# A two-layer attention and expert kernel on one core: the order of each engine's steps written anew

## The chip, the cores and the metric

The kernel runs on 1 core of one Trainium2 chip. The metric is the device time of one execution in microseconds (us). A core has five engines that run side by side, each its own list of instructions in order: TensorE (PE, matrix products), VectorE (DVE), ScalarE (ACT), GpSimd (POOL), and SyncE (SP), which here only starts transfers (DMAs). They meet through semaphores: an instruction waits until a count is reached, and adds to one when it ends.

## The reference

```python
x = x + L0_xattn(layernorm(x), ctx)   # 16 heads of 8: q, k with an RMS norm per head, softmax, values, projection
x = x + L0_ffn(layernorm(x))          # int8-like quantised input, 128 -> 512, 3-tap conv along the sequence, silu, 512 -> 128
x = x + L1_xattn(layernorm(x), ctx)   # one head of 128, then a product with [x, output]
x = x + L1_ffn(layernorm(x))          # 8 experts: softmax(x @ gate); (silu(x @ Wg) * (x @ Wu)) @ Wd, weighted by the gate
```

x is 64 sequences of 128 rows of 128 float32 values, ctx 64 of 120 rows of 128. With 128 rows and a capacity of all of them, each expert takes every row.

## The kernel before

The 64 sequences go through in 16 groups of 4 (`SIZES`). Each group passes six stages, and a stage is a fixed list of steps on each engine (`steps_of`, L339):

- **n**: first layer norm (POOL: `ln1` = three small operations, L945, and `xn1` = four of L955), its transpose, q, k and v on PE (L565 to L586), the RMS roots on DVE (`rms` 1 to 9, L1066 and L1072 to L1079), then the copies `k_r` to `ql` on DVE (L1174 to L1197), `k_hi` on ACT (L840) and `dup_q`, `dup_k` on POOL (L975, L981). SP then transposes `kht`, `qht` and `ks` (L471 to L483) and spreads `kht` into `kbd` with 16 small DMAs for the first two sequences (`kbd0`).
- **m**: 16 steps `max`, four per sequence: one matmul into the only bank BM (L597), one reduction on DVE (L1202). SP's step of this stage (`kbd1`, L500) is the 16 DMAs for the other two sequences. A `max` of sequence 0 waits for its quarter of `kbd0`, one of sequence 2 for its quarter of `kbd1`.
- **a**: per sequence `stacks`, two `scores`, `values`, `turn` on PE with ACT copies and exponentials between them, and on DVE `rden` and `turn`; then `ont` and `proj`. POOL's step is `xres` (L991), which needs the input `xres` from a DMA.
- **b**: the feed-forward part: `quant` 0 to 4 on DVE (L1238 to L1251), transpose `xit`, four `fc1`, conv and silu, four `h2t`, and `fc2`, which waits for four DMA transposes `hit` (L517).
- **d**: the second attention: `xn3t`, `bf`, `s1`, `p1t`, `oc`, `fused`, `xn4t`, `gate` on PE.
- **c**: the experts, in 16 units: PE `g` (three matmuls into bank pg), `u` (three into pu), ACT tanh of pg (L915) and copy of pu (L931), DVE product (L1363, step `u`), POOL product (L1000, step `u`), PE `d` (L783), DVE sum (L1377). Bank pg is single: the next `g` waits for L1363 of the unit before.

**w** is the preparation of the weights, once: on DVE `wabs`, `wint`, `gate_w`, `wg`, `wu` (L1107 to L1135).

How the stages of different groups mix is written out by hand, as a string per engine in `ORDER`: each letter means "the next step of that stage" (`run`, L402), so a string fixes the engine's whole order, and within one stage the order never changes. In the middle part c of group g runs beside d of g+1, b of g+2, a of g+3 and m and n of g+3 to g+5; the strings repeat with a period of some 108 PE steps, one group. Before the first c there is only the rest to do (the fill), and at the end only c is left (the tail). `UNREAD` says at which of PE's steps, counted from 0, so many float32 products of 128x128 are made that nobody reads (L790); each shows as two matmul records in the trace.

Of the kernel before, what the change touches and what calls it, by code (L numbers as in the profile page):

```python
# [64 lines left out]
STAGES = "wnmabdc"  # L65
ORDER = {
    "sp": (
        "annnnmnnnnnnnnnmnnnnannmnbbnnnbbnanmdbbnbnnbnnanmdbbnbnbcnnnanmdbbbbncnnnnamdnbbbbnnnmcadnnnbbbbnnncamdnnnbb",
# [8 lines left out]
        "dbmcamccabcmccabnnmdacacdmbcmcccbcmccbamccamccbmccamccaaccbamccamcanaccaccdaadccdccccaccdccdcdbcaccbancabann",
        "mcbcdmcccdbccmaccacmcbaccaacbcamccabmccmccbmacmcaaccamccbamccamnamccaccdaadmccdmccmccaccdccdcdbcaccbancabann",
        "ccbdmcccdbccamccacmcbamccaacbcamccabmcccmcbamccaaccamccbamccamnamccaccdaadmccdmccmccamccdccdcdbcaccbancabann",
        "ccbdccmcdbccamccacmcbamccaacbcamccabmcccmcbamccaaccamccbamccamnamccaccdaadmccdmccmccamccdccdcdbcaccbancabann",  # L80
        "ccbdccmcdbccamccacmcbamccaacbcamccabmcccmcbamccaaccamccbamccamnamccaccdaadmccdmccmccamccdccdcdbcaccbancabann",
        "ccbdccmcdbccamccacmcbamccaacbcamccabmcccmcbamccaaccamccbamccamnamccaccdaadmccdmccmccamccdccdcdbcaccbancabann",
        "ccbdccmcdbccamccacmcbamccaacbcamccabmcccmcbamccaaccamccbamccamnamccaccdaadmccdmccmccamccdccdcdbcaccbancabann",
        "ccbdccmcdbccamccacmcbamccaacbcamccabmcccmcbamccaaccamccbamccamnamccaccdaadmccdmccmccamccdccdcdbcaccbancabann",
        "ccbdccmcdbccamccacmcbamccaacbcamccabmcccmcbamccaaccamccbamccamnamccaccdaadmccdmccmccamccdccdcdbcaccbaccabacc",
        "dcbcdccambccmcaccambcaacambcamccbmccmccabmcaccaccamcbamccamcamccacdadaccdmccmccamccdcmdccdbcaccbaccabaccdcbc",
# [10 lines left out]
        "ccdbcacbancbbabcnbdccncbbccadbcacacbcbacabcbcccbabcacbbaccacaccannaccdadcccdccacdccdbcacbancbbabcnbdccncbbcc",
        "adbcacacbcbacabcbcccbabcacbbaccacaccannaccdadcccdccacdccdbcacbancbbabcnbdccncbbccadbcacacbcbacabcbcccbabcacb",
        "baccacaccannaccdadcccdccacdccdbcacbancbbabcnbdccncbbccadbcacacbcbacabcbcccbabcacbbaccacaccannaccdadcccdccacd",
        "ccdbcacbancbbabcnbdccncbbccadbcacacbcbacabcbcccbabcacbbaccacaccannaccdadcccdccacdccdbcacbancbbabcnbdccncbbcc",  # L100
        "adbcacacbcbacabcbcccbabcacbbaccacaccannaccdadcccdccacdccdbcacbacbcbacdbcbcccbbacdcabcacababcbcbccabcbcacbbca",
# [18 lines left out]
        "ddbcdcbbacbbabmnbnbdbcdmbdnbcbmdnbccbdbdbmcanannnbnbnbcmnnnbmbnbcmnnbmbcbmncaacmcbmddmamanncncnabmbcdmdcmddb",  # L120
        "cbbcbcbddbcdcbbacbbabnnbnbdbcdmdnbbcbdmdbcdmcbmbnbncanannbnbnbcmnnnbmbnbcmnnbcbmbcaacmcbmddmamanncncnabmbcdm",
        "dcmddbcbmbcbcbddbcdcbbacbbabnnbnbdbcdmdnbbcbdmdbcdmcbmbnbncanannbnbnbcmnnnbmbnbcmnnbcbmbcaacmcbmddmamanncncn",
        "abmbcdmdcmddbcbmbcbcbddbcdcbbacbbabnnbnbdbcdmdnbbcbdmdbcdmcbmbnbncanannbnbnbcmnnnbmbnbcmnnbcbmbcaacmcbmddmam",
        "anncncnabmbcdmdcmddbcbmbcbcbddbcdcbbacbbabnnbnbdbcdmdnbbcbdmdbcdmcbmbnbncanannbnbnbcmnnnbmbnbcmnnbcbmbcaacmc",
        "bmddmamanncncnabmbcdmdcmddbcbmbcbcbddbcdcbbacbbabnnbnbdbcdmdnbbcbdmdbcdmcbmbnbncanannbnbnbcmnnnbmbnbcmnnbcbm",
        "bcaacmcbmddmamanncncnabmbcdmdcmddbcbmbcbcbddbcdcbbacbbabnnbnbdbcdmdnbbcbdmdbcdmcbmbnbncanannbnbnbcmnnnbmbnbc",
        "mnnbcbmbcaacmcbmddmamanncncnabmbcdmdcmddbcbmbcbcbddbcdcbbacbbabnnbnbdbcdmdnbbcbdmdbcdmcbmbnbncanannbnbnbcmnn",
        "nbmbnbcmnnbcbmbcaacmcbmddmamannccabmbcdmdcmddbcbmbcbcbddbcdcbbcbaabbcdbdbdbcmbbmbcdcbcdmbdbabambbbmcbmbbcmbc",
        "babamccmcbmddmamaccabbcdmdcmddbcbmbcbcbmddbcdcbbcbaabbcdbdbdbcbbcbcbcddbababdbbbcbbbcbbbcccaabdcdaaccabbccdd",
# [1287 lines left out]
```

How the kernel before makes its waits and increments, by code:

```python
            def do_n(name, t, c, g):  # L458
                n = size(g)
                if name == "xin" and g < NG - 1:
                    sp.wait_ge(xn1_done.sem, xn1_done.at(g))
                    sp.dma_start(xin[:, 0:size(g + 1), :], x_g(g + 1)).then_inc(xin_in.sem, 16)
                elif name == "ctxa" and g < NG - 1:
                    sp.wait_ge(v_ps.sem, v_ps.at(g))
                    sp.dma_start(ctxt_a[:, 0:size(g + 1), :], ctxt_g(g + 1)).then_inc(ctxa_in.sem, 16)
                elif name == "kht":
                    sp.wait_ge(kh_done.sem, kh_done.at(g))
                    if later(g):
                        for part in kbd_in[0] + kbd_in[1]:
                            sp.wait_ge(part.sem, part.at(g - 1, 16 * HQ))
                    sp.dma_start_transpose(kht[:, 0:n, :], heads(k_hi[:, 0:n, :])).then_inc(kht_in.sem, 16)
                elif name == "qht":
                    sp.wait_ge(q_hi_done.sem, q_hi_done.at(g))
                    if g >= 2:
                        sp.wait_ge(max_ps.sem, max_ps.at(g - 2, 4 * size(g - 2)))
                    sp.dma_start_transpose(qht2[:, g % 2, 0:n, :], heads(q_hi[:, 0:n, :])).then_inc(qht_in.sem, 16)
                elif name == "ks":
                    sp.wait_ge(dup_done.sem, dup_done.at(g, 2))
                    sp.wait_ge(kl_done.sem, kl_done.at(g))
                    if g >= 2:
                        sp.wait_ge(s_ps.sem, s_ps.at(g - 2, 2 * size(g - 2)))
```

## Time and profile before

| | |
|---|---|
| three runs | 1236.44, 1240.61 (median), 1243.52 us |
| the profiled execution | 1241.86 us, of it a span of 1239.9 us from the first to the last instruction |
| PE busy | 1118.7 us, 90% (of it unread products 53.7) |
| DVE busy | 1038.1 us, 84% |
| ACT busy | 836.3 us, 67% |
| POOL busy | 700.4 us, 56% |
| idle of PE in the first 62 us | 42.6 us |

A row of a group of instructions names the line, the engine, the operation, what is written and what is read, how many there are, the busy time and the mean of one in ns. `x4` in a timeline row means four instructions merged. What stands in square brackets is the idle time of the engine just before, and who ended it. DVE and ACT rows that follow each other can overlap by 0.1 us.

### The profile page before, as it was taken

The page shows a single profiled execution, that of the slowest core. Times are in us where ns is not written, and L with a number is a line of the kernel's source. Part 1 is how long each engine was busy: PE and PEld are TensorE (multiplying, and loading weights), DVE is VectorE, ACT ScalarE, POOL GpSimd, SP SyncE. Part 2 cuts the span into 40 slices and gives each one's busy share as a digit, 9 for nine tenths or more (in the row PEclk, how much of TensorE's full clock was granted, in tenths as well). Part 3 has the DMA queues.
Part 4 walks back from the last instruction along what each step waited for, and adds up shares of the span by engine and source line. Part 5 has one row for each costly group of instructions (what it writes and reads, how often), then busy time and mean ns, then how long its engine had stood idle before and what let it go on. Part 6 is the DMA issues. An engine that isn't in the chain of part 4 may idle for free.

```text
span 1239.9 us, 27832 instructions
## 1 busy us (share of the span) xinstructions
PE 1118.7 (90%) x10025; PEld 806.6 (65%) x10025; DVE 1038.1 (84%) x2728; ACT 836.3 (67%) x1685; POOL 700.4 (56%) x827
## 2 busy tenths in 40 slices
...
DMA packets 151399, 53.67 MB, mean 43 GB/s; under 512 B 116832, under 2 KB 150624, under 8 KB 150880
## 3 DMA queue, kind: packets, MB, share of 16 engines
...
q14 instruction: 54, 0.44, 0.1%
...
## 4 chain that ended last, share of the span: by engine, by line
DVE 38%; PE 32%; POOL 10%; issue 7%; ACT 6%; SPq 4%; DMA 2%; POOLq 0%; DVEq 0%
PE py L783 5%; DVE moe L1363 5%; DVE q_st L1202 5%; POOL xn L955 4%; SPq L498 3%; DVE h L1272 2%; DVE acc L1377 2%; DVE am L1277 2%; PE pa L633 2%; POOL moe L1000 2%; DVE xn L1251 2%; DVE cv L1266 2%; PE pg L773 2%; DVE cv L1261 2%; DVE rr L1079 2%
## 5 line engine op out<-in xcount | busy, mean ns | idle before, releaser
L1000 POOL TENSOR_TENSOR moe<-moe 128x512 f32<-128x512 f32 x256 | 331.4, 1296 | 369.1 <-ACT moe L931 223.6
L783 PEld LDWEIGHTS py<-wd_s,moe 128*128 128x128 f32 x1856 | 236.8, 192 | 28.4 <-DVE acc L1377 6.2
L783 PE MATMUL py<-wd_s,moe 128*128 128x128 f32 x1856 | 246.6, 277 | 4.1 <-DVE acc L1377 3.7
L1363 DVE SCALAR_TENSOR_TENSOR moe<-tg,pg 128x512 f32<-128x512 f32 x232 | 157.8, 680 | 41.0 <-ACT tg L915 39.0
L1202 DVE TENSOR_REDUCE q_st<-pa 128x4 f16<-128x480 f32 x256 | 168.0, 656 | 24.2 <-PE pa L597 24.1
L915 ACT ACTIVATE tg<-pg 128x512 f32<-128x512 f32 x232 | 139.5, 602 | 60.9 <-PE pg L775 58.5
L849 ACT ACTIVATE probs<-pa 120x512 f32<-120x512 f32 x256 | 139.5, 605 | 24.2 <-PE pa L623 24.0
L931 ACT ACTIVATE moe<-pu 128x512 f32<-128x512 f32 x232 | 140.7, 606 | 11.3 <-PE pu L775 8.6
L597 PE MATMUL pa<-kbd,qht 128*128 128x480 f16 x256 | 96.1, 375 | 20.9 <-DMA kbd<-kht 10.7
L773 PE MATMUL pg<-x4h,wg_h 128*128 128x512 f16 x232 | 88.8, 383 | 17.2 <-DVE moe L1363 17.0
L955 POOL TENSOR_SCALAR xn<-x,lnm,lnr 128x128 f32<-128x128 f32 x192 | 101.6, 542 | 1.5
L773 PE MATMUL pu<-x4h,wu_h 128*128 128x512 f16 x232 | 88.2, 380 | 0.0
L775 PE MATMUL pg<-x4h,wg_l 128*128 128x512 f16 x232 | 88.2, 380 | 0.0
L774 PE MATMUL pg<-x4l,wg_h 128*128 128x512 f16 x232 | 88.2, 380 | 0.0
L774 PE MATMUL pu<-x4l,wu_h 128*128 128x512 f16 x232 | 87.9, 379 | 0.0
L775 PE MATMUL pu<-x4h,wu_l 128*128 128x512 f16 x232 | 87.9, 379 | 0.0
L633 PE MATMUL pa<-probs,v_st 120*9 120x128 f32 x2048 | 70.0, 275 | 1.0 <-ACT probs L849 0.5
L950 POOL TENSOR_TENSOR lnr<-lnv,half 128x4 f32<-128x4 f32 x64 | 66.3, 1036 | 0.0
L873 ACT ACTIVATE hr<-pb,magic,sc 128x512 f32<-128x512 f32 x64 | 49.9, 780 | 24.1 <-DVE sc L1283 23.6
L633 PEld LDWEIGHTS pa<-probs,v_st 120*9 120x9 f32 x2048 | 49.3, 91 | 19.1 <-issue 14.3
L597 PEld LDWEIGHTS pa<-kbd,qht 128*128 128x128 f16 x256 | 24.9, 97 | 56.7 <-DVE q_st L1202 17.8
L1377 DVE SCALAR_TENSOR_TENSOR acc<-py,aff,acc 128x128 f32<-128x128 f32 x208 | 58.2, 341 | 3.8 <-PE py L783 3.7
...
## 6 DMA issues: line engine op xcount, KB each, us to landing
kbd<-kht SPq DMA_DIRECT2D x512, 3.8 KB
...
```

The lines of the kernel that those rows point to most:

```text
L633: mm = pe.matmul(pa[32 * n:32 * n + HD + 1, BO, i * S:(i + 1) * S], v_st[0:SC, t, HQ * n + i, :], probs[0:SC, i, n, :], start=True, stop=True)
L773: pe.matmul(o, w_hi[:, us], x4h, start=True, stop=False)
L774: pe.matmul(o, w_hi[:, us], x4l, start=False, stop=False)
L775: pe.matmul(o, w_lo[:, us], x4h, start=False, stop=True).then_inc(done.sem, 1)
L783: mm = pe.matmul(moe_y(g, e)[:, j, :], hu[:, u % 3, j * S:(j + 1) * S], wd_s[:, u, :], start=(half == 0 and j == 0), stop=(half == 1), ski ...
L849: act.activation(probs[0:SC, i, :, :], pa[0:SC, i % 2, :], ACT.Exp).then_inc(p_done.sem, 1)
L915: act.activation(tg[:, u % 2, 0:wide], moe_bank("g", g, u)[:, 0:wide], ACT.Tanh, scale=0.5 / WSCALE)\
L931: act.activation(us[:, u % 3, 0:wide], moe_bank("u", g, u)[:, 0:wide], ACT.Copy, scale=0.5 / WSCALE ** 2)\
L955: ins = pool.tensor_scalar(dst[:, j, :], src[:, j, :], lnm[:, i, j:j + 1], lnr[:, i, j:j + 1], ALU.add, ALU.mult)
L1000: pool.tensor_tensor(hu[:, u % 3, 0:wide], gw[:, u % 3, 0:wide], us[:, u % 3, 0:wide], ALU.mult)\
L1202: dve.tensor_reduce(q_st2[:, g % 2, t, 4 * c:4 * c + 4, 3 * HD], pa[:, BM, 0:4 * SC].rearrange("p (h k) -> p h k", h=4), AX.X, ALU.max, ne ...
L1363: dve.scalar_tensor_tensor(out=gw[:, u % 3, 0:wide], in0=tg[:, u % 2, 0:wide], scalar=1.0, in1=moe_bank("g", g, u)[:, 0:wide], op0=ALU.add ...
```

## The change

All ORDER strings are replaced, and UNREAD is: 162 unread products in 59 places become 166 in 53, the last of them before PE's step 158 and not 165. No instruction of the computation is added or dropped: PE keeps its 1731 steps, ACT 1300, POOL 496, DVE 1845, SP 224. What is different in them, read off with `steps_of`:

- POOL at the start: `ln1, xres, xn1, dup_q, dup_k` of group 0 becomes `ln1, xn1, dup_q, dup_k`; `xres` of group 0 comes after `xn1` of group 2.
- DVE at the start: `wabs` before `ln1`; `gate_w` goes between the roots of group 0, `wg` to after `qb` of group 1, `wu` to after the last `max` of group 0. In the string of before all of these stand ahead of `qb` of group 0.
- SP at the start: `kht, qht, kbd1, ks, kbd0` of group 0 becomes `kht, qht, ks, kbd0, xin, ctxa, kbd1`.
- PE: `stacks` of group 0 comes after 10 of its `max` steps and not after 4; the first `max` comes before k and v of group 1.
- The first `g` is PE's step 162 and not 168, the second group's 284 and not 285, then (before/after) 393/392, 504/510, 609/619, and the last group's 1683/1682.
- In the middle, `proj` to `xit` of a group is 24 PE steps before and 60 after; `fc2` to `xn3t` 15 and 50; from the step ahead of ACT's `k_hi` to the first `max` of the same group 52 and (groups 8 to 11 and 13) 37. SP's order there differs from group to group: groups 8, 9, 10, 13 and 15 have `kbd1` before `ks` and `kbd0`, with `kht` just ahead of it or `qht` between; the others have `kbd0` first.
- In the middle the steps between `g` of unit 1 and `g` of unit 2 were `u, s1, max`; now they are `u, turn, stacks`.

```diff
--- before.py
+++ after.py
@@ -40,7 +40,7 @@
-UNREAD = {1: 2, 2: 3, 3: 3, 4: 3, 6: 3, 7: 3, 8: 3, 11: 3, 12: 3, 13: 3, 14: 3, 15: 3, 16: 3, 18: 3, 20: 1, 32: 3, 34: 3, 37: 2, 39: 3, 41: 3, 43: 2, 46: 2, 48: 3, 50: 3, 52: 1, 58: 3, 59: 3, 60: 3, 62: 3, 64: 3, 66: 3, 74: 3, 75: 3, 76: 2, 84: 3, 88: 3, 90: 1, 94: 3, 98: 3, 100: 3, 102: 2, 109: 3, 113: 3, 116: 2, 117: 3, 118: 3, 119: 3, 120: 3, 129: 3, 131: 3, 133: 3, 135: 3, 144: 3, 148: 3, 153: 2, 158: 3, 161: 3, 163: 3, 165: 2}
+UNREAD = {1: 4, 2: 3, 3: 4, 4: 3, 7: 4, 8: 3, 11: 4, 12: 4, 14: 4, 15: 4, 16: 4, 17: 3, 18: 3, 19: 3, 25: 3, 27: 4, 31: 2, 33: 3, 35: 4, 39: 2, 41: 3, 43: 4, 47: 2, 49: 3, 51: 4, 59: 4, 60: 3, 63: 4, 65: 2, 70: 2, 71: 3, 78: 3, 81: 3, 88: 3, 92: 4, 95: 3, 100: 2, 102: 3, 113: 4, 115: 3, 118: 3, 119: 3, 121: 4, 123: 2, 126: 3, 128: 2, 135: 3, 138: 3, 139: 1, 142: 4, 147: 2, 156: 3, 158: 3}
...
@@ -65,69 +65,69 @@
     "sp": (
-        "annnnmnnnnnnnnnmnnnnannmnbbnnnbbnanmdbbnbnnbnnanmdbbnbnbcnnnanmdbbbbncnnnnamdnbbbbnnnmcadnnnbbbbnnncamdnnnbb",
-        "bbnnncamdnnnbbbbnnncamdnnnbbbbnnncamdnnnbbbbnnncamdnnnbbbbnnncamdnnnbbbbnnncamdnnnnbbbbnncaamdnnbbbbcdbbbbcd",
-        "dbbbcbcc",
+        "nnnnnnnnmnnnannmnannnnmbbnnnnbbnnmbbbndbnnannnmbbbnnabncnadnnmdbbbbnnnnnnmacbbndbbnnnmnncbnbbbandnmannncbnbb",
+        "nbdnmnannnnbdcbbbnnmnnbbannbcbanndnnmbbbnbcncndnnnmbndabnbbnmnnnnbabcbnbcndnnnmbbanbbnncdmnnnbadbbbbcbdbbcbb",
+        "bdbcdacc",
     ),
     "pe": (
-        "wwwnnnnnnnnmmmmaammamamnaanmnmamammamaaammamamaaammamamnammaaaamamnamnaanmmmbmambamambaaambamambaaamambamnab",
-        "mabaaambammmmnmbnmnmaaamamadadmadabmmbamdmbdmdbmaabaaamdmbmdccambcamcbanmccbaccaaccaccacbccccanmcanncaccamcc",
...
+        "wwwnnnnnnmnmmnmmmmmmnmnnaamamamaaamamamaaamamamaaamamamnmamamammnanmnmamaambaabmamaabmaambamabmmamambaambama",
+        "mbnambamammmbnannmamaadmadadmbmbmadmbdmdbmaambaaammdmbcdmccabmacbaaccabccacamnaccabcaaccaccacamccaaccacmccdm",
...
     ),
     "act": (
-        "wwwwnnnnnnnnnnaaaanannaaaaaaaaaaannaaaanaanbnabaabbaabbaabbaabaabnbbabnabababbnaannaadadabdbadbbdbbaabbaabdc",
...
+        "wwnwwnnnnnnnnnnaanaanaaaaaaaaaaaannananaanababaabababbabbaabababababnnbbabbnannaaaddabdbadbbdbbaabbaabdcbbdc",
...
     ),
     "pool": (
-        "nannnnnnnnnnnnanbbnnnnadbdbdddncccncncncabcbdcddcccccccncddccnccnncabcbdcddcccccccddccnccccccdnccdbcbcdcancn",
-        "cdcdcccccccccdcddccanbcbccncnncddcccccccccnccdcddccabcbcncncncddcccccccccnccdcddccabcbcncncncddcccccccccnccd",
...
+        "nnnnnnnnnnannnnabbnnnnaddbbdddccncnccadbcbcdndcccncccddcccccccccddcbacbcncncnccndcddcccccccnnccdaccbdbcnccnd",
+        "ccddccccccccccbbdcccdcndnccncnccddccccccaccdcacbbccccndncndccncccddcccccccdccabcbccncdccncdnncccddcccccccdca",
...
     ),
     "dve": (
-        "nwnwwwwnnnnnnnnnnnnnnnnnnnnnnnnnnnnnnnnnnnnnnnnmmmmnnmmmmaanmnmnmnnmnnmnnmnnanannmnmnmnmaammmmamanmnnnabbmmm",
-        "nbababmbmbmnmbmnnbmbmnbababmnnbbmbmnbababmnbmnbnbnbmnnababmbnnnbbnbnnbmbnbmmmmmbmadbdbmnanamnnmnnnnnbnbnbnbm",
...
+        "wnnwnnnnnnnwnnnnnnnnnnnnnnnwnnmnnnnnnmnnnnnnnmnnnmnmnmmmmmnnmnmmannnnnmanmnmwnmanammnnnnnaammmmannamnnmambmb",
+        "nmnbbmbnbmbnmnnbnannanmnnbnbmnbmbabmbabbmnmbbmbmbmbbbaambnbbmbmbabamnnbbbnmnmnmmbadbdnbnmnnnnnnnmmbbanbbbndm",
...
     ),
```

## Rows read from the trace of the kernel before

**Rows 1.** The page: busy time of each engine.
```profile
PE 1118.7 (90%) x10025; PEld 806.6 (65%) x10025; DVE 1038.1 (84%) x2728; ACT 836.3 (67%) x1685; POOL 700.4 (56%) x827
```
**Rows 2.** Stretches: length; busy (count) of PE, PEld, DVE, ACT, POOL; PEclk; DMA; GB/s.
```profile
34.30:194.90 160.60, 125.84 (x1263) 97.82 (x1264) 128.07 (x333) 74.05 (x134) 43.48 (x69) 0.91 0.20 46
155.00:186.00 31.00, 26.41 (x282) 19.44 (x283) 29.71 (x84) 16.13 (x34) 8.84 (x16) 1.00 0.16 39
556.80:626.50 69.70, 66.32 (x608) 47.23 (x609) 63.52 (x171) 51.66 (x106) 43.67 (x52) 1.00 0.22 42
768.90:841.30 72.40, 66.40 (x608) 47.09 (x608) 63.75 (x171) 51.68 (x106) 43.62 (x52) 1.00 0.20 44
```
**Rows 3.** What PE waited for, whole span: us in total, times, longest.
```profile
PE pa L565 <- POOL xn L955: 21.7, 2, 12.4
PE pg L773 <- DVE moe L1363: 17.0, 33, 1.1
PE pa L597 <- DMA kbd<-kht: 10.7, 5, 6.2
PE pb L664 <- DVE xn L1251: 7.5, 13, 1.7
```
**Rows 4.** Timeline of POOL and DVE at the start (start, length).
```profile
18.57 1.03 POOL L950 TENSOR_TENSOR lnr<-lnv,half 128x4 f32<-128x4 f32 x1
22.93 1.26 POOL L991 TENSOR_TENSOR xres_b<-xres,bp_s 128x512 f32<-128x512 f32 x1 [3.33 <-DMA xres<-in_x]
24.18 5.96 POOL L955 TENSOR_SCALAR xn<-xin,lnm,lnr 128x128 f32<-128x128 f32 x4
...
26.34 2.28 DVE L1135 SCALAR_TENSOR_TENSOR wu_l<-moe,wu_h 128x2048 f16<-128x2048 f32 x1
```
**Rows 5.** Timeline of SP, groups 0 and 1.
```profile
45.46 11.79 SPq L498 DMA_DIRECT2D kbd<-kht  x16
...
59.08 11.65 SPq L498 DMA_DIRECT2D kbd<-kht  x16
```
**Rows 6.** Timeline of PE and DVE: the first `max` steps, the first `stacks`, `proj` of group 0.
```profile
63.13 0.58 PE L597 MATMUL pa<-kbd,qht 128*128 128x480 f16 x1 [6.25 <-DMA kbd<-kht]
73.51 0.63 PE L609 MATMUL pa<-id_h,q_st 128*128 128x128 f16 x4
107.38 1.16 PE L654 MATMUL pa<-wp_s,on_t 128*128 128x128 f32 x8
...
77.31 0.66 DVE L1202 TENSOR_REDUCE q_st<-pa 128x4 f16<-128x480 f32 x1 [0.47 <-PE pa L597]
```
**Rows 7.** Timeline and two stretches around the longest wait in the middle.
```profile
353.18 3.71 DVE L1242 TENSOR_SCALAR am<-am 128x4 f32<-128x4 f32 x1
...
355.60 1.27 POOL L991 TENSOR_TENSOR xres_b<-xres,bp_s 128x512 f32<-128x512 f32 x1
...
359.31 0.61 PE L623 MATMUL pa<-st_t,ks_t 32*128 32x128 f16 x8 [2.96 <-ACT p L895]
...
361.00:366.00 5.00, 5.00 (x43) 2.59 (x42) 3.17 (x6) 2.25 (x5) 2.92 (x5) 0.55 0.03 5
```
**Rows 8.** Two groups of DVE instructions: busy us, mean ns; then idle before.
```profile
L1242 DVE TENSOR_SCALAR am<-am 128x4 f32<-128x4 f32 x16 | 15.2, 947 | 0.0
L1280 DVE TENSOR_SCALAR am<-am 128x1 f32<-128x1 f32 x64 | 9.3, 145 | 0.3
```
**Rows 9.** Timeline: one hand-over of bank pg.
```profile
497.95 0.68 DVE L1363 SCALAR_TENSOR_TENSOR moe<-tg,pg 128x512 f32<-128x512 f32 x1
...
498.68 0.39 PE L773 MATMUL pg<-x4h,wg_h 128*128 128x512 f16 x1 [0.44 <-DVE moe L1363]
498.91 0.38 PE L774 MATMUL pg<-x4l,wg_h 128*128 128x512 f16 x1
...
499.54 0.60 ACT L915 ACTIVATE tg<-pg 128x512 f32<-128x512 f32 x1 [0.66 <-PE pg L775]
```
**Rows 10.** DMA issues: how many, median us from issue to landing.
```profile
kht<-k_hi SPq DMA_TRANSPOSE x16, 2.4
```

More of the change, by code:

```diff
@@ L77 @@
[L77 to L86, printed above, removed]
@@ new lines @@
+        "cacbcacadbcdnaabdccamcbmacannaadbcccdmccbamccambanacmcbaccaacmamcbcmccmcacmccamcacaccacmcdmcdmccmdcccbmcccbm",
+        "ccamcbadncmdbaacdbcaccamamnanbacdmccbccmdcmcabmcacmbacnacmcccacbacacmacamamcaacamccacaccaaccaccbdccbdcccdbcc",
+        "cacabdnaacdmbcdcmacbmacmancbmnamdcbcadcaaccambcccmaccmccmcbmccccmncmcccmamcaacaccamaccaaccaccacabaacbacccdbc",
+        "dccdbccccbccamanccdmabdcmdbacnmanbmnccdacbccdmcamccmccmbccacmccmccmcccmamcaacmaccamaccaacaccacabcaacbacccdbc",
+        "cdcdbccccbccamaccndmabdcmdbacnnmabmnccdacbcdcmcamcccmcbcmccmcacmccmcccmamcaacmaccamaccaacaccacabcaacbacccdbc",
@@ new lines @@
+        "cdcbcdccccbcamancdcamdbcmdbacnmnambnccdacbcdcmcamccmccmbcccamccmccmcccmamcaacmaccamacacaccaccaabcaacbacccdbc",
+        "dccdbcccccbcamaccdnambdmcdbacnnmabmnccdcbacdcmcamccmccabcmccmccmccmcccmamcaacaccamacmcaaccaccacabcaabacccdbc",
+        "dccdbcccmbccacadccmandbcmdbacnmnabmnccdcbacdcmcamccmccbcmccamccmccmcccmamcaacamccamaccaaccacacabcaacbacccdbc",
+        "dccbcdccbccacmacdcnmdabcmdbacnmnabmnccdacbccdmcamccmccbmcccamccmccmcccmamcaacmaccamaccaaccaccacabaacbacccdbc",
+        "dccdbcccccbcamaccdnmbdmacdbacnmanbmnccdcabcdcmcamccmccbcmccmcacmccmcccmamcaacmaccamacaaccaccacabcaacbacccdbc",
@@ L89 @@
+        "cdcccbdcccbccamcadcdambdcabcmcacbcccmcbadccmcdcamccmbcacccmcccmamcaaccacmcacadcmdaacdmcccbmccmbaccacmabcdaac",
+        "dbccdbcaccacaccbdacbdcaccacbcccccbccccccccbcccccccccccccccccbcccbdcccdbcccdccccbcccdcccbdccdcbccccbccccbdccc",
+        "dcbcccccccccbccccccccccdccccdccdccccccdccdccccdccccccccccdccccccccdccccccccccccccccccccccccccccccccccccccccc",
         "ccc",
@@ L97 @@
[L97 to L101, printed above, removed]
@@ new lines @@
+        "bbcaabacnacbdbcnccbcdabbaccbabncbccaccacaaanacaccacaccacacbdcbdccbcdbcacbabdnacbdbbcacabccabnbdcbcanabdcbcac",
+        "bcbccccaccccnccaaacacacncaccaacabacbaccbdbcdcbbccbdbcaccbadndccbacbbnbnncbdbcacbdbcaccccccccacccaaacacacncac",
+        "acacabcabaccbdbcdcbbccbdbcaccbadccdnbbacbnnbncbdaccbbdbcaccccccacccccaaacacacnaccacacabacbaccbdbcdbbcccbdbca",
+        "acbdcdcnbcbacbnnbncbdaccbbdbcacccccaccccccaaacacacncaccaacabcabaccbdbcdcbbccbdbcacabcdcdncbacbbbnnncbdbcacbd",
+        "cbaccccacccccccaaacacaccaccanacabcabaccbdbcdbcbccbdbcacabdcdcbbcnacbnbnncbdbcacbdbcaccccccacccccaaacacacncac",
@@ L104 @@
+        "acacabcabaccbdbcdbbcccbdbcacbadcdncbcacbbnnbncbdacbcbdbcaccccccacccccaaacacaccnaccacacababaccbdbcdbcbccbdbca",
+        "cabdccdnbbcacbnbnncbdcacbbdbcaccccccacccccaaacacacnaccacacabcabaccbdbccdbcbccbdcbacdbacdbcabcbcbccbcbcadbcbc",
+        "cdcaccaccccaacaccadaccdacccbdcabcababdccbadbccbbaccabccacdbbdacbbcccbcbcccbcbccccccccccccccccbcbcdccbbdccdbc",
+        "cbcccdbcccbdcbccbccbcbccbdcbccdbcbbcccccccccccdccdcccccdcdcccdcccccccccccdcccccdcccccccccccccccccccccccccccc",
         "cccc",
@@ L120 @@
[L120 to L129, printed above, removed]
@@ new lines @@
+        "bcbbbdaamdbdmbcbnbnnbdbcbndmdncbnbabmacdnbnbmncnabdnamnnbbbndnncnmmnbmccdmdcanmcmbbcancmacnmbbbmbmcbccdbmcdb",
+        "mbdmdbbbmcbaabbcdbdbbdmcmbncbabbnanmdbbcmdbdnmcbbbmnnnbndbmdbcnaandcmcnncbanbmndbdmnnmcncnnaabcnbbmcbbcancbc",
+        "bbcaddbcbbddbcbbacmbbbdabmmbdbdbmncbmbbanmadcdbbndbcnndncnbmbbncnnmmdcdnmcmbcmcnddmacmbnmabacncnmbcbnabcabnn",
+        "bcnbncbnbcaabbcbcdbbcbdbbdbcdmbmbbaabmcdbdbcdbmnnbmbnbncdbbcbddmnndmcndndmncbmdcmcmcadmcnnmbmnbaacmncmnncbaa",
+        "nbcbbnbnncbncbbncbbacbcdbbcbdbaddcbbmbmcbbabamdbdbcdbnmnbmbnbncdbcbnbddmdnnmcnndmdncbmdcmcmcndmacnmbmbnnanam",
```

34 lines of the change are left out of this document (16 added, 18 removed).

## The prediction

> **What bounds the kernel now.** First the busy times [rows 1]: PE works 90% of the span, and the change takes no matmul away. What can be gained is the 121 us in which PE is idle, and the 53.7 us of unread products, which only stand where PE would wait. Then the stretches [rows 2]. In the fill (34.3 to 194.9) DVE is busy 128.1 of 160.6 us and PE 125.8, much of it unread products; from 155 to 186 DVE is busy 29.7 of 31 us. In the middle both are near full: PE 66.3 and DVE 63.5 of a period of 69.7 us. So in the middle no order can save more than 3.4 us a period; but the same order repeated gives one period of 72.4 us with the same 66.4 us of PE work. Third, PE's waits [rows 3]. The largest is at the start, 21.7 us for POOL's `xn1` of groups 0 and 1. Then come many small ones on DVE's hand-over of bank pg (17.0 in 33), waits for `kbd` (10.7 in 5), and `xit` waiting for `quant` (7.5 in 13).
>
> Two places show what the two engines do to each other. At 24.18 POOL's four `xn1` operations take 5.96 us, while DVE runs two operations of 2.28 us, the second of them shown [rows 4]. At 353.18 a DVE operation on four numbers per partition takes 3.71 us, while POOL runs on from one operation to the next, one of them the `xres_b` at 355.60 [rows 7]; that form's mean is 0.95 us [rows 8]. PE then waits 2.96 us, and afterwards a stretch of 5 us runs at a granted clock of 0.55, which is about the lower of the two levels, 1.2 GHz [rows 7].
>
> The Trainium skill (SBUF — State Buffer, section "SBUF: two separate sides") says that VectorE and GpSimd share a port pair which the one that starts first holds for its whole instruction. It would hold the tiny operation back for what was left of one GpSimd operation. The trace disagrees in size: the wait went over three of POOL's, the last of them ending at 356.87. By the rule the stall at 353 would be some 1.3 us and not 3.6, and the term for it below about -1 in place of -4.
>
> **The change, term by term**, against the profiled execution's 1241.9 us (span 1239.9; the median of the three runs, 1240.6, is 1.3 lower).
>
> 1. *Start.* POOL's roots end at 19.60; `xn1` then stood behind `xres`, whose DMA was late, until 24.18, and behind DVE's `wg` and `wu`, until 30.14 [rows 4]. With `xres` moved behind and `wg`, `wu` moved to later, `xn1` starts at about 20.5 (DVE's `ln1` now comes after `wabs`, I allow 0.9) and ends at about 24, 6 us earlier. The cover is gone for `wg` and `wu`: their 4.6 us on DVE now stand beside groups 1 and 2. ACT's two weight copies come between `xn1t` and `qsq`; I allow 0.4.
>    On SP `kbd1` of group 0 took 11.79 us ahead of `ks` and `kbd0` [rows 5]. Now `ks` can go at about 40 and `kbd0` at 42, and 4.05 us later (59.08 to 63.13 in rows 5 and 6) PE's first `max` starts: at 46, not 63.1.
>    That isn't a gain of 17. `stacks` of group 0 now comes after ten `max`; the ninth and tenth need `kbd1`, issued behind `kbd0` and two inputs from about 55, so 62 by SP. By DVE it is later: in its order group 1's roots and copies, `wg` and the ten `max` (1.13 us from one to the next, the 0.66 and 0.47 of rows 6) stand ahead: I count 71, against 73.5 [rows 6], 2.5 earlier. From there to `proj` (33.9 us before [rows 6]) there are 15 `max` and not 20, up to 0.66 us each: 3.3, of which I take 2.5. DVE has done the same work by `proj` of group 0 in both orders, and from there to the first `g` it is nearly full, so what is gained there stays. Term: **-5**. Bounds: -12 if SP decides (stacks at 62), and -1 if DVE's later `wu` and `wg` use the gain up.
> 2. *The stall at 353.* Without it PE's 2.96 us wait goes, and of 5 us at 0.55 [rows 7] the 2.3 us that the lower clock cost. In the new string `quant` of that group stands beside other POOL steps. Term: **-4**, bounds 0 (it comes up elsewhere) and -6. What is late next is the hand-over of pg.
> 3. *Other blocking in the middle.* The tiny L1242 takes 0.95 us where one like it, L1280, takes 0.15 [rows 8]: 16 times 0.8 is 13 us of held DVE, and other operations on SBUF alone are held too. Only where PE waits for DVE is it worth anything. Going by the two periods, 69.7 and 72.4 [rows 2], I take **-2**, bounds -7 (three slow periods gone) and +3 (one more).
> 4. *More room before `xit` and `xn3t`.* `proj` to `xit` goes from 24 PE steps to 60 and `fc2` to `xn3t` from 15 to 50, at 69.7/108 = 0.65 us a step 23 and 22 us more. The 7.5 us of waits for `quant` [rows 3] have no reason left in the middle. Term: **-4**, bounds 0 and -7.5.
> 5. *Less room for bank pg.* From the end of `g` to the next `g` the chain needs 0.16 (0.39 less the 0.23 from one start to the next), 0.60 on ACT, 0.68 on DVE and some 0.1 between them, 1.55 us [rows 9]. With `u, turn, stacks` between, PE has 0.66 for `u` and an estimated 0.44 and 0.22 for the other two (512 columns each, the first in float32, at twice the price), 1.3 us of work: 0.25 short, once a period, and in some groups twice. I take 0.3 in 13 groups: **+4**, bounds 0 (ACT and DVE are late anyway) and +6.
> 6. *Unread products.* Four more, 53.7/162 = 0.33 us each, 1.3 us at most; they stand in waits for `kbd` and in group 0. **0**, bounds 0 and +1.3.
> 7. *The rest:* PE's own step counts to the second and last `g` differ by one, and the tail has only c in it: 0. SP's changed places I cost at nothing; their cover is the first rival.
>
> Sum: -5 - 4 - 2 - 4 + 4 = -11, so 1241.9 - 11 = **1231 us**.
>
> **Rivals.**
> *A, slower: `kbd` late in the middle.* In groups 8, 9, 10, 13 and 15 SP issues `kbd1` ahead of `ks` and `kbd0`, and PE's distance from the `k_hi` to the first `max` shrinks from 52 steps to 36 to 38: 23.9 us, not 33.5. Needed are 2.4 for `kht` to land [rows 10], 11.8 for `kbd1`, 1.8 for each of `qht` and `ks` (the gap between the two `kbd` rows, 57.25 to 59.08, in which `ks` was issued), and 4.05 to the first quarter of `kbd0` [rows 5, 6]: 21.9. The margin is 2 us. It decides as soon as something holds SP by more, since SP's queue is in order and stands behind `ctxa` and the `hit` steps. A wait of 3 us and 1 us for the clock after it, five times, is +20: 1251. For it: PE already waited for `kbd` 10.7 us in all [rows 3]. Against it: `kht` goes long after the `hit` steps before it.
> *B, nothing gained:* the start's gain is used up by DVE, which is full in the fill [rows 2], and the waits only change places: term 1 at -1, 2 to 4 at -4 together, 5 at +4: 1241. For it: 63.5 of 69.7 us of DVE [rows 2].
> *C, more:* SP decides at the start (-12), the stall and all slow periods go (-6 and -7), pg costs nothing and `xit`'s waits go by half: sum -12 - 6 - 7 + 0 - 4 = -29 at its end; half-way between this and the forecast, 1221. For it: the places named are where POOL and DVE meet.
> That the order on the chip isn't the one in the strings can't be: each engine runs its list in order.
>
> **How the numbers follow.** Forecast 0.50, with a range of its own of 1223 to 1238; A 0.14; B 0.21; C 0.15. This kernel's runs can tell 0.5% (6.2 us) from no change, so faster is under 1234.4, slower over 1246.8. Faster: all of C, and 0.42 of the forecast's 0.50: 0.57. Slower: A, 0.14. The rest 0.29. The range 1216 to 1247 leaves out A's centre and C's far end.
>
> **What would show it.** Term 1: PE's first `max` near 46 us, `xn` L955 of group 0 under 4 us, `proj` of group 0 (107.4) near 102. Term 2: no DVE operation of over 3 us, no stretch at a clock of 0.55 after 100 us. Term 3: L1242's mean under 0.6 us. Term 4: `pb L664 <- xn L1251` under 3 us. Term 5: `pg L773 <- moe L1363` stays at 15 or more. A: waits of `pa L597 <- kbd` of 2 us and more after 600 us. The prediction is wrong if periods of the middle are over 71 us on the mean, or if the first `g` comes no earlier than before.

## The result and the profile after

| | median | runs |
|---|---|---|
| before | 1240.51 us | 7, 1236.44 to 1244.42 |
| after | 1232.37 us | 7, 1230.12 to 1234.82 |

The ratio is 0.9936, 95% interval 0.9914 to 0.9959: 8.1 us shorter, faster by the bound of 0.5%. The forecast was 1231. The profiled execution took 1234.4 us with a span of 1232.5.

The page of the changed kernel, busy time of each engine, against [rows 1]:

```profile
PE 1122.8 (91%) x10033; PEld 805.9 (65%) x10033; DVE 1043.8 (85%) x2728; ACT 836.8 (68%) x1685; POOL 695.4 (56%) x827
```

Stretches of the changed kernel, columns as in [rows 2]: the fill up to the first product of the experts, the first stretch of DVE near its limit, and the two periods that answer to those of before:

```profile
34.30:186.50 152.20, 121.34 (x1182) 91.16 (x1182) 125.56 (x316) 69.29 (x125) 41.17 (x68) 0.93 0.20 42
155.00:186.00 31.00, 26.05 (x252) 17.43 (x253) 29.07 (x72) 18.61 (x38) 9.66 (x19) 1.00 0.02 4
552.30:628.80 76.50, 68.77 (x609) 49.00 (x607) 66.80 (x171) 51.89 (x105) 44.16 (x52) 0.96 0.21 40
768.80:839.00 70.20, 66.58 (x611) 46.56 (x607) 64.24 (x170) 51.73 (x105) 44.38 (x52) 1.00 0.25 51
```

The first product of the experts comes 8.4 us earlier. The period that took 72.4 takes 70.2, but the one that took 69.7 takes 76.5, at a mean clock of 0.96: a stall that before didn't have. From the start of the span to that first product, before and after:

```profile
0.00:194.88 194.88, 135.00 (x1302) 106.42 (x1304) 143.48 (x364) 80.11 (x140) 57.86 (x87) 0.90 0.27 71
0.00:186.48 186.48, 135.74 (x1251) 104.42 (x1251) 147.37 (x360) 76.94 (x134) 53.29 (x86) 0.93 0.27 68
```

PE is idle for 59.9 us of it before and for 50.7 after, 9.1 less. Over the whole span its idle time falls from 121.2 to 109.7 us, 11.5 less, and its busy time grows by 4.1. So in these two executions only 2.4 us of the idle time saved lie behind the first product.

What PE waited for, against [rows 3]:

```profile
PE pb L664 <- DVE xn L1251: 15.7, 14, 2.5
PE pa L597 <- DVE q_st L1202: 13.9, 20, 2.9
...
PE pa L565 <- POOL xn L955: 13.1, 2, 11.1
PE pg L773 <- DVE moe L1363: 12.7, 16, 3.2
```

The start's wait fell from 21.7 to 13.1 and that for `kbd` from 10.7 to 1.9 in two. The wait for bank pg fell too. The wait of `xit` for `quant` (L1251), which was to go, has doubled, and that of `max` for DVE's reduction (L1202) grew from 9.0 us to 13.9.

The start of the changed kernel, POOL and DVE, against [rows 4]:

```profile
19.29 2.67 POOL L955 TENSOR_SCALAR xn<-xin,lnm,lnr 128x128 f32<-128x128 f32 x4
...
21.68 7.00 DVE L1125 TENSOR_SCALAR w_i<-hr 128x512 f16<-128x512 f32 x1
21.91 6.49 POOL L970 MEMSET kbd<- 128x7680 f16 x1
```

`xn1` is 2.67 us long and ends 8 us earlier. But POOL's clearing of the `kbd` tiles now lies beside DVE's L1125, which takes 7.00 us; its twin at 20.23 took 0.56. SP and then PE, against [rows 5, 6]:

```profile
41.81 11.81 SPq L498 DMA_DIRECT2D kbd<-kht  x16
...
58.07 11.65 SPq L498 DMA_DIRECT2D kbd<-kht  x16
```

```profile
47.43 0.37 PE L597 MATMUL pa<-kbd,qht 128*128 128x480 f16 x1
...
70.44 0.39 PE L609 MATMUL pa<-id_h,q_st 128*128 128x128 f16 x4
...
101.32 1.23 PE L654 MATMUL pa<-wp_s,on_t 128*128 128x128 f32 x8
```

The first `max` is 15.7 us earlier, `stacks` 3.1 and `proj` 6.1.

### Where the middle gave it back

The stall at 353 is gone, with its stretch at 0.55 [rows 7]. Around 604 the changed kernel has another. SP's queue, ACT, DVE and PE there, and the stretch behind it:

```profile
596.84 1.22 SPq L517 DMA_TRANSPOSE hi_t<-hq  x1
598.11 0.58 SPq L523 DMA_DIRECT2D ctxt_b<-in_ctx_t  x1
598.73 2.02 SPq L524 DMA_DIRECT2D ctxn_b<-in_ctx  x1
600.80 0.46 SPq L528 DMA_DIRECT2D out_x<-acc  x1
601.31 6.39 SPq L517 DMA_TRANSPOSE hi_t<-hq  x3
...
605.76 0.72 ACT L881 ACTIVATE hq<-hr,unmagic 128x512 f16<-128x512 f32 x1 [2.06 <-DMA hi_t<-hq]
...
607.00 0.69 DVE L1363 SCALAR_TENSOR_TENSOR moe<-tg,pg 128x512 f32<-128x512 f32 x1 [2.05 <-ACT tg L915]
...
607.74 0.61 PE L773 MATMUL pg<-x4h,wg_h 128*128 128x512 f16 x1 [3.18 <-DVE moe L1363]
```

```profile
608.00:616.00 8.00, 8.00 (x43) 5.39 (x42) 5.54 (x17) 3.49 (x9) 3.75 (x3) 0.65 0.05 9
608.00:613.00 5.00, 5.00 (x26) 3.23 (x25) 3.07 (x9) 2.54 (x7) 3.50 (x3) 0.50 0.07 15
```

To be read upwards: PE waits 3.18 us for the product that frees bank pg; DVE waits for ACT's tanh; ACT's tanh stands behind `hq`, which waits for a `hit` transpose to release its buffer. SP had put three transfers between the first transpose and the second, which went at 601.31 and not at about 598.1. PE did not work for 3.18 us, and then ran 8 us at a granted clock of 0.65, the first 5 of them at 0.50, the lower of the two levels. The periods, of both kernels in their profiles: from the first unit of group 3 to that of group 10 the changed kernel takes (910.3 - 409.1)/7 = 71.6 us a period, the kernel before (910.9 - 418.5)/7 = 70.3. Some 0.5 us of this difference is no loss: by the strings PE has 757 steps between these two points and had 752, at 0.65 us a step.

### The profile page after: what moved, and what is told of

Same layout as the page of the kernel before. It is cut to its first block, busy times and chain, and to the rows that moved or that the text cites. A ratio compares the mean times of both kernels' runs of the same rounds, so it can differ in the third digit from the quotient of the medians.

```text
span 1232.5 us, 27848 instructions
## 1 busy us (share of the span) xinstructions
PE 1122.8 (91%) x10033; PEld 805.9 (65%) x10033; DVE 1043.8 (85%) x2728; ACT 836.8 (68%) x1685; POOL 695.4 (56%) x827
## 4 chain that ended last, share of the span: by engine, by line
PE 57%; DVE 28%; ACT 6%; issue 3%; SPq 2%; POOL 2%; DMA 1%; POOLq 0%; DVEq 0%; ACTq 0%
PE py L783 11%; PE pg L773 3%; PE pa L597 3%; DVE moe L1363 3%; DVE q_st L1202 3%; PE pg L775 3%; PE pg L774 3%; PE pu L773 3%; PE pu L775 3%; PE pu L774 3%; PE pa L633 3%; DVE xn L1251 2%; PE pb L680 2%; ACT probs L849 2%; DVE h L1272 2%
## 5 line engine op out<-in xcount | busy, mean ns | idle before, releaser
L783 PEld LDWEIGHTS py<-wd_s,moe 128*128 128x128 f32 x1856 | 236.4, 192 | 26.5 <-issue 3.9
L783 PE MATMUL py<-wd_s,moe 128*128 128x128 f32 x1856 | 250.1, 278 | 3.0 <-ACT side L927 1.7
L1202 DVE TENSOR_REDUCE q_st<-pa 128x4 f16<-128x480 f32 x256 | 168.0, 656 | 24.8 <-PE pa L597 23.0
L597 PE MATMUL pa<-kbd,qht 128*128 128x480 f16 x256 | 95.5, 373 | 17.4 <-DVE q_st L1202 13.9
L773 PE MATMUL pg<-x4h,wg_h 128*128 128x512 f16 x232 | 89.3, 385 | 14.2 <-DVE moe L1363 12.7
L955 POOL TENSOR_SCALAR xn<-x,lnm,lnr 128x128 f32<-128x128 f32 x192 | 97.2, 518 | 2.6 <-POOL lnr L950 0.7
L633 PE MATMUL pa<-probs,v_st 120*9 120x128 f32 x2048 | 75.1, 274 | 5.2 <-ACT probs L849 1.4
L947 POOL TENSOR_SCALAR lnv<-mv 128x4 f32<-128x4 f32 x64 | 14.3, 224 | 113.3 <-DVE mv L1090 110.2
L975 POOL TENSOR_SCALAR q_st<-q_hi 128x1024 f16<-128x1024 f16 x16 | 19.4, 1211 | 88.3 <-DVE q_hi L1186 88.3
L633 PEld LDWEIGHTS pa<-probs,v_st 120*9 120x9 f32 x2048 | 44.1, 90 | 34.9 <-ACT probs L849 14.9
```

Source lines behind the costliest of these rows:

```text
L597: pe.matmul(pa[:, BM, 0:4 * SC], qht2[:, g % 2, t, :], kbd[:, t, 4 * c:4 * c + 4, :], start=True, stop=True).then_inc(max_ps.sem, 1)
L633: mm = pe.matmul(pa[32 * n:32 * n + HD + 1, BO, i * S:(i + 1) * S], v_st[0:SC, t, HQ * n + i, :], probs[0:SC, i, n, :], start=True, stop=True)
L773: pe.matmul(o, w_hi[:, us], x4h, start=True, stop=False)
L783: mm = pe.matmul(moe_y(g, e)[:, j, :], hu[:, u % 3, j * S:(j + 1) * S], wd_s[:, u, :], start=(half == 0 and j == 0), stop=(half == 1), ski ...
L1202: dve.tensor_reduce(q_st2[:, g % 2, t, 4 * c:4 * c + 4, 3 * HD], pa[:, BM, 0:4 * SC].rearrange("p (h k) -> p h k", h=4), AX.X, ALU.max, ne ...
```

## The experiments

The experiments ran on three chips, and the kernel before had medians of 1243.55, 1238.05 and 1245.22 us there. So each kernel is compared with those that ran on the same chip, and where two chips are compared it is said.

**The two halves of the change.** `newfill` has the new strings and unread products up to the first unit of the first experts stage and the old ones behind, `oldfill` the converse:

```diff
 # newfill: UNREAD of after, and of each engine's string
+    the first SP 35, PE 162, ACT 103, DVE 256, POOL 30 steps of after
     then the steps of before that are left, in before's order
 # oldfill: UNREAD of before, and of each engine's string
+    the first SP 37, PE 168, ACT 107, DVE 261, POOL 31 steps of before
     then the steps of after that are left, in after's order
```

> The changed kernel's orders and unread products up to the first unit of the first expert stage, and the orders of the kernel before behind it. Theory (the whole gain lies in the fill: first DVE unit at 186.5 instead of 194.9 us, and from there to the end both kernels take 1037 us): 1233 to 1236 us, first unit near 186.5, and the stall at 353 us still there, because the old middle comes with its own orders. Rival (the new middle is needed, the fill alone brings work forward that waits later): 1239 to 1241 us.

> The converse: the fill of the kernel before and the changed kernel's orders behind it. Theory (gain in the fill): 1239 to 1241 us, first unit near 194.9, no stall at 353 but the one at 604 to 608 us. Rival (the middle is worth part of the gain): 1235 to 1237 us.

Measured: newfill 1241.11 against 1243.55 us (ratio 0.9966, 0.9944 to 0.9989), oldfill 1237.87 (0.9944, 0.9922 to 0.9966). So my theory that the fill alone carries the gain fell on this chip: both halves gain against the kernel before, and the middle 5.7 us of it, though the two intervals overlap. newfill's first unit came at 192.3 and not at 186.5, since at the seam its old strings still had steps to make up; so it is no clean measure of the fill. It has the stall at 353, oldfill the one at 604, as expected.

**The start, POOL, DVE and ACT alone.** SP's residual load moves back with POOL's step.

```diff
 # before, first steps
-    POOL: n.ln1 a.xres n.xn1 n.dup_q n.dup_k n1.ln1 ... n2.xn1
+    POOL: n.ln1 n.xn1 n.dup_q n.dup_k n1.ln1 ... n2.xn1 a.xres
-    DVE:  n.ln1 w.wabs n.ln1_mv w.wint w.gate_w w.wg w.wu n.qb ...
+    DVE:  w.wabs n.ln1 n.ln1_mv w.wint n.qb ... gate_w among group 0's roots; wg, wu as in after
-    ACT:  w.bvt w.gate_w w.wg w.wu n.xn1t
+    ACT:  w.bvt w.gate_w n.xn1t w.wg w.wu
```

> The kernel before with the changed order of the first steps on POOL, DVE and ACT alone: POOL's residual of group 0 behind its norm of group 2 instead of ahead of the first one, DVE's weight preparations behind the first norm's steps, ACT's wg/wu copies behind the first xn1 transpose; SP's residual load moves back with it, its block-diagonal loads stay where they were. Theory (the step sized 5 us in the prediction, which measured 8.4 us at the first unit together with SP's part): the first maximum comes 3 to 6 us earlier, the time 3 us shorter than before, 1237 to 1238 us. Rival (the order of SP's loads bounds the start, and the two engines alone only wait for them): first maximum within 1 us of 63.1, time 1240 to 1241 us.

Measured: 1241.03 against 1243.55 us (0.9968, 0.9942 to 0.9993). The first DVE reduction `max` came at 58.9 and not 65.1 and the first unit at 188.4 and not 194.9. So these three engines, with SP's one load, bring 6.5 us at the first unit, but only 2.5 at the end in front of the old middle. In the trace the lead is 6.5 us at group 1's first unit, 4.0 at group 2's, 2.4 at group 9's and 1.3 at the end.

**The clearing moved.**

```diff
+            pool.memset(kbd[:, :, :, :], 0.0)    # first on POOL
-                    if g == 0:                     # after xn1 of group 0
-                        pool.memset(kbd[:, :, :, :], 0.0)
```

> The changed kernel with POOL's clearing of the block-diagonal tiles at its very start, so that it does not lie beside DVE's half-precision copy of the projection weights, which took 7.00 us there instead of 0.43. Theory (GpSimd's 6.49 us clearing holds that copy, and q waits for it): copy under 1 us, q's preparation 3 us earlier, time 2 to 4 us shorter than the changed kernel, 1229 to 1231 us. Rival (the first norm on POOL starts later by the clearing's time, or SP's loads bound the first maximum anyway): 1232 to 1235 us.

Measured: 1232.91 us; the changed kernel has 1232.37 and 1231.88, the second of them on another chip than this. DVE's L1125 takes 0.57 us again, `qb` starts at 26.5 and not 28.7, the first reduction `max` at 50.2 and not 51.6; the first unit at 186.4 and not 186.5. So the copy is freed, as expected, and nothing is gained. But the edit took away something that the changed kernel mostly doesn't have. In its second profile (the next experiment) the copy starts 0.82 us ahead of the clearing and keeps its length:

```profile
20.92 0.56 DVE L1125 TENSOR_SCALAR w_i<-hr 128x512 f16<-128x512 f32 x1
...
21.74 6.49 POOL L970 MEMSET kbd<- 128x7680 f16 x1
```

There `qb` starts at 25.7, the first reduction `max` at 49.7 and the first unit comes at 184.4, and the span is 2.4 us shorter (1230.1). The six other profiles of kernels with this start on POOL and DVE and the clearing in its place have no hold either. So the 7.00 us belong to one profiled execution, and this experiment couldn't price them. What they cost there is not shown; the first units of the two profiles lie 2.1 us apart.

**The changed kernel again.**

> The changed kernel itself, unaltered, beside the others of this call, because the split of the change in two halves gave 0.34% for the new fill and 0.56% for the new middle, and the early clearing 1.04%, all on another chip than the changed kernel's own 0.64%. Theory (the halves add up): ratio to before 0.990 to 0.992. Rival (they overlap): 0.993 to 0.995.

Measured: 1231.88 against 1238.05 us, 0.9951 (0.9935 to 0.9967). That is just outside the rival's range, on its side: the halves overlap by this, 0.49% for the whole. But the changed kernel has the same time both times (1232.4 and 1231.9), and the kernel before, over its four medians, has not. The spread goes the same way: every kernel with the old middle spreads over 8 to 15 us (before 8.0, 11.7, 10.7, 12.9; newfill 9.9; startpool 14.9; swap_stall 8.8, in 7 to 26 runs), and those with the new middle and unread products over 2 to 5 (5 to 9 runs; some of the difference is that they are fewer). The last experiment, with the new middle and no unread products, spreads over 9.7 in 12. That is seen in times alone, without two profiles of one kernel from both ends of it, so its mechanism stays open.

**The stall at 353 by one exchange on DVE.**

```diff
 # before, DVE, group 4's quant beside group 3's s1
-    b4.quant1 d3.s1 b4.quant2 d3.nmax b4.quant3
+    d3.s1 d3.nmax b4.quant1 b4.quant2 b4.quant3
```

> The kernel before with one exchange on DVE: the copy of the second scores of the cross attention of group 3 and its negated maximum go ahead of the second step of group 4's quantisation, so that the small operation of L1242 that was held for 3.71 us no longer stands ahead of them. Theory (PE's wait of 2.96 us at 353 us and the clock of 0.55 behind it are one event, caused by that order; the new middle's worth of 0.56% is mostly this): PE wait there under 0.5 us, clock 1.0 in 361 to 366 us, group 3 starts 4 to 6 us earlier relative to group 2, and the time 3 to 5 us shorter, 0.996 to 0.9975 of before. Rival (DVE is the bound there and gives the gain back in the same period): period of group 2 to 3 shorter by under 1.5 us and time within 1.5 us of before.

Measured: 1237.66 against 1238.05 us, 0.9997 (0.9983 to 1.0011): nothing. DVE and POOL of this kernel there, and PE's wait:

```profile
353.55 0.68 DVE L1363 SCALAR_TENSOR_TENSOR moe<-tg,pg 128x512 f32<-128x512 f32 x1
354.14 0.65 DVE L1311 TENSOR_REDUCE nmax<-pa 128x4 f32<-128x480 f32 x1
354.83 3.02 DVE L1315 TENSOR_SCALAR nmax<-nmax 128x4 f32<-128x4 f32 x1
357.76 0.16 DVE L1242 TENSOR_SCALAR am<-am 128x4 f32<-128x4 f32 x1
```

```profile
352.88 1.27 POOL L1000 TENSOR_TENSOR moe<-moe 128x512 f32<-128x512 f32 x1
354.11 1.27 POOL L1034 TENSOR_TENSOR x2b<-x,a2b_s 128x512 f32<-128x512 f32 x1
355.33 1.27 POOL L1000 TENSOR_TENSOR moe<-moe 128x512 f32<-128x512 f32 x1
356.56 1.26 POOL L991 TENSOR_TENSOR xres_b<-xres,bp_s 128x512 f32<-128x512 f32 x1
```

```profile
359.50 0.40 PE L623 MATMUL pa<-st_t,ks_t 32*128 32x128 f16 x8 [2.19 <-ACT p L895]
```

L1242 is no longer held: 0.16 us. The hold went to L1315, the next tiny DVE operation on SBUF, which ends when POOL's unbroken row of four ends at 357.8. In between a product that reads a bank (0.68) and a reduction of a bank (0.65) went through at their usual length. This points to POOL's row as the cause, and not to DVE's order; no run changed the row itself. PE still waits 2.19 us; the clock stays at 1.00 from 361 to 366, and the period is 76.0 us and not 78.7. The profiled execution ended 4.4 us before the one of before, the medians 0.4: between my two cases in the trace, and with the rival in the times.

**The h tiles first.**

```diff
 # after, SP
-    b7.hit0 d6.ctxb c4.out b7.hit1 b7.hit2 b7.hit3
+    b7.hit0 b7.hit1 b7.hit2 b7.hit3 d6.ctxb c4.out
```

> The changed kernel with SP's loads of the cross attention's context of group 6 and the output of group 4 behind the last transposed h tile of group 7 instead of between its first and second one. Theory (these transfers hold the transpose's DMA, ACT waits 3.4 us for it, tg comes late, DVE and PE stop near 605 us and the clock falls to 0.65): PE wait of 3.2 us gone, the period from group 5 to group 6 near 72 us instead of 76.5, time 3 to 5 us shorter than the changed kernel. Rival (context or output late instead, or DVE takes the time back): period shorter by under 1.5 us, time within 1.5 us of the changed kernel.

Measured: 1228.27 us (1226.76 to 1228.94) against 1231.88 (1230.33 to 1234.85) for the changed kernel, whose ranges don't touch: 3.6 us. SP's queue and two stretches of this kernel, the period and the 8 us of the stall:

```profile
594.96 8.09 SPq L517 DMA_TRANSPOSE hi_t<-hq  x4
603.10 0.58 SPq L523 DMA_DIRECT2D ctxt_b<-in_ctx_t  x1
```

```profile
550.40:621.30 70.90, 65.93 (x609) 47.27 (x607) 66.07 (x171) 51.70 (x105) 44.17 (x52) 1.00 0.19 43
...
608.00:616.00 8.00, 7.69 (x81) 5.43 (x79) 8.00 (x22) 5.21 (x12) 6.90 (x8) 1.00 0.01 2
```

The period is 70.9 and not 76.5 us, PE's busy time in it 65.9 and not 68.8 at a clock of 1.00: some 2.8 us of the stall were the lower clock and 2.8 the waiting. At the end 3.6 of these 5.6 us are left. The longest wait for pg is 1.5 us and not 3.2.

**Both.** The two edits together.

> The changed kernel with both the early clearing and the SP order of the run that puts the h tiles first. Theory (independent places, both on the path): the sum of the two differences, 4 to 7 us shorter than the changed kernel, 1226 to 1229 us. Rival (the early clearing is worth nothing at the end, as the profiled runs of 1232.5 and 1231.5 us say): the same as with the h tiles first alone, within 1 us.

Measured: 1229.57 us (1227.19 to 1230.44), with hit_first at 1228.27: the clearing brings nothing here either, and hit_first's own profile has no hold that it could take away (L1125 takes 0.56 us).

**The worth of the fill, on a quiet middle.** The control is hit_first once more; `hitoldfill` has before's fill (and UNREAD) ahead of it.

```diff
 # hitcontrol: after with the h tiles first
-    162 steps of PE (and the like on the others) of after, UNREAD of after
+    168 steps of before, UNREAD of before
```

> The changed kernel with the h tiles first, again, as the control of the other three of this call. Theory: as before, 1227 to 1230 us.

> The fill and the unread products of the kernel before, behind it the changed kernel's orders with the h tiles first; against its control only the fill differs, and both have the same middle. Theory (the new fill is worth 0.3 to 0.6% also where the middle is quiet; its first unit comes 8.4 us earlier, 5.5 us of it at equal work of PE): 4 to 6 us longer than the control. Rival (the middle gave the larger part, 0.56% against 0.34% in the split on the other chip, and the fill's lead is partly given back): 1 to 3 us longer.

Measured: control 1228.93 us (0.9863 of before, 0.9836 to 0.9890), hitoldfill 1234.23 (0.9911, 0.9887 to 0.9935); the ranges, 1225.9 to 1229.8 and 1233.1 to 1235.6, don't touch. The fill is worth 5.3 us. The first unit comes 9.0 us apart, that of group 1 5.3 us: the rest was only PE's other steps moved behind.

**xit moved behind.** Groups 6 to 13, the same edit in each:

```diff
 # control, PE, group 7
-    c5.g3 a8.values2 b7.xit c5.u3 a8.turn2 a8.stacks3 c5.d1 b7.fc1 a8.scores3
+    c5.g3 a8.values2 c5.u3 a8.turn2 a8.stacks3 b7.xit c5.d1 a8.scores3 b7.fc1
```

> The control with PE's transposes of the second norm (xit) of groups 6 to 13 behind the turn and the stacks of the attention that stood behind them, and the first projection behind the last scores. PE waits 15.7 us for DVE's xn at xit in all, about 1.1 us a group. Theory (PE is the bound and these waits are on its path; the order gives it 1 us of other work there): wait under 6 us, time 3 to 8 us shorter than the control. Rival (DVE, ACT and the convolution behind xit are the bound, and what comes later there is late everywhere): same waits elsewhere (cv, xh, turn), time from 1 us shorter to 6 us longer.

Measured: 1226.86 us against 1228.93, ranges 1225.3 to 1228.2 and 1225.9 to 1229.8: 2.1 us at the median, which the overlap leaves unclear. PE's waits of this kernel:

```profile
PE pb L664 <- DVE xn L1251: 6.0, 9, 2.0
PE pa L623 <- ACT st_t L845: 5.6, 8, 1.7
```

9.5 us of waits went (the control has 15.5 us of the first kind), and 5.6 us of another kind are there instead, for the stacks that ACT copies. The theory gets the wait (6.0, at its bound of 6), not the time, which fell short of its 3 us; the rival had the waits coming back elsewhere right.

**No unread products.**

```diff
-UNREAD = {1: 4, 2: 3, 3: 4, ...}
+UNREAD = {}
```

> The control without the unread products of the fill, which no result uses. Theory (the prediction's step of 0: they only hold the clock up; without them TensorE's granted clock falls in the first 190 us where PE waits): the clock under 0.9 in several stretches of the fill, first unit 3 to 15 us later, time 3 to 15 us longer. Rival (PE is busy enough by itself in the fill): within 1.5 us of the control.

Measured: 1242.25 us (1235.52 to 1245.21), 13.3 above the control. A stretch of the fill of this kernel, up to its first unit, and of the control, up to its own:

```profile
30.00:196.20 166.20, 104.23 (x884) 64.46 (x885) 128.92 (x328) 69.36 (x126) 41.55 (x68) 0.75 0.18 40
```

```profile
34.30:185.60 151.30, 121.56 (x1182) 91.25 (x1182) 124.04 (x314) 69.44 (x125) 41.33 (x68) 0.93 0.20 42
```

The granted clock is 0.75 and not 0.93, and the first unit comes at 196.2 and not at 185.6. This is the worth of all of them together. The profiled execution was the fastest of the twelve, 8.3 us above the control's, so the trace shows less than the medians. What the new places of the change are worth against the old ones was not tried alone.

## Right and wrong, point by point

The sum was -11 us; the medians gave -8.1, the two profiled executions -7.5 (1241.9 to 1234.4). The start and the stall at 353 were right in place, two wrong terms of the same size cancelled, and a stall that no term had took part of the gain. That the sum came so near is luck in this part: for the start it is not, but terms 2 to 5 were to bring -6 and brought half of that or less, as counted below.

1. *Start, -5 (-12 to -1).* Right. `xn1` under 4 us (2.67), first `max` near 46 (47.4), `stacks` at 71 (70.4), `proj` near 102 (101.3); the fill is worth 5.3 us. DVE's order, not SP's, decided as counted. The 7.00 us of the held L1125 was not in the sum; the second profile of the same kernel doesn't have it, and its first `max` comes at 45.4.
2. *The stall at 353, -4.* It is gone from its place, and the clock is 1.00 from 361 to 366. But two of the signs failed. "No stretch at a clock of 0.55 after 100 us": from 608 to 613 it is 0.50. "No DVE operation of over 3 us": the 7.00 at the start, in this execution. And the bound "it comes up elsewhere" came true in another form, at 604, of nearly the same price (3.6 us by hit_first). That the price of 353 was 4 us is not shown: the exchange on DVE left 2.19 of 2.96 us of the wait, took the low clock away, and moved the median by 0.4.
3. *Other blocking, -2.* L1242's mean is under 0.6, as said:

```profile
L1272 DVE SCALAR_TENSOR_TENSOR h<-th,cv 128x512 f32<-128x512 f32 x64 | 56.0, 875 | 6.7 <-ACT th L870 6.3
L1251 DVE TENSOR_SCALAR xn<-xn,am 128x128 f32<-128x128 f32 x64 | 32.5, 570 | 0.1
...
L1242 DVE TENSOR_SCALAR am<-am 128x4 f32<-128x4 f32 x16 | 8.5, 533 | 0.3
```

   But L1251 had 490 ns before and has 570, L1272 743 and now 875; DVE's busy time didn't fall (1038.1 to 1043.8; the control, without the 7.00, has 1035.6). The blocking moved to other operations. I had read one operation and taken it for all.
4. *More room before `xit`, -4.* This is the step that failed: "The 7.5 us of waits for `quant` have no reason left in the middle." They are 15.7. The room was counted on PE, and it did come: from `proj` to `xit` of group 6 it is 16.1 us before and 38.8 after. Both kernels there, PE's `proj`, DVE's own `proj` step (L1224), its last `quant` step, PE's `xit`, the kernel before first:

```profile
488.02 1.06 PE L654 MATMUL pa<-wp_s,on_t 128*128 128x128 f32 x8
...
489.11 0.69 DVE L1224 TENSOR_TENSOR x<-pa,xres_b 128x512 f32<-128x512 f32 x1 [0.47 <-PE pa L654]
...
502.17 1.89 DVE L1251 TENSOR_SCALAR xn<-xn,am 128x128 f32<-128x128 f32 x4
...
504.11 0.66 PE L664 MATMUL pb<-id_f,xn 128*128 128x128 f32 x4 [0.24 <-DVE xn L1251]
```

```profile
455.15 1.06 PE L654 MATMUL pa<-wp_s,on_t 128*128 128x128 f32 x8
...
475.12 0.68 DVE L1224 TENSOR_TENSOR x<-pa,xres_b 128x512 f32<-128x512 f32 x1
...
492.14 1.76 DVE L1251 TENSOR_SCALAR xn<-xn,am 128x128 f32<-128x128 f32 x4
...
493.95 0.66 PE L664 MATMUL pb<-id_f,xn 128*128 128x128 f32 x4 [1.74 <-DVE xn L1251]
```

   DVE takes its `proj` step 20.0 us after PE's, where it took it 1.1 us after. All the new room lies ahead of DVE's step, and none between it and `xit` but 3.8 us, which other DVE steps fill. I should have measured it in DVE's string. The other half of the term came true: the kernel before waited 2.6 us for POOL's `xn` at `xn3t` (L721), the changed one doesn't.
5. *Less room for pg, +4 (0 to +6).* Wrong: 12.7 us in 16 and not 17.0 in 33; without the stall at 604 9.9 in 16. The sign, 15 or more, wasn't met, and the 0.25 us that I found missing doesn't show as a wait per period. The two errors, -4 and +4, cancel in the sum, and that is luck.
6. *Unread products, 0*: not tested; all of them together are worth 13.3 us, the four more were not tried alone. 7. *The rest, 0*: SP's places, priced at nothing but for the rival on `kbd`, were not nothing. The stall at 604 is SP's order, 3.6 us, of another kind than the rival's.

The rivals: A (`kbd` late) is out, 1.9 us of waits in two. B came true in the middle: with the fill at 5.3 us, terms 2 to 5 and the stall at 604 together are left with -2.8 us of the first difference (-8.1) and -0.9 of the repeated one (-6.2), with the 5.3 taken over from the experiment on a quiet middle (oldfill, against a kernel before that was slower on that chip, had -5.7); the start kept it from coming true as a whole. C is out. The sign that periods over 71 us on the mean would show the prediction wrong was met, 71.6, by the one stall (70.8 and 70.4 in the two profiles without it): it was a bad sign to choose, since the time was right all the same.

The best version is the control with `xit` behind, 1226.9 us, 0.9852 of before (0.9822 to 0.9881); 3.6 us of its lead over the changed kernel are secured, by two letters moved in one string.
